# Attention scores from two fp32r parts, with two heads' products side by side in row tiles

## The chip, the cores and the metric

The kernel runs on one core of one Trainium2 chip. The metric is device time in microseconds (us). The kernel before was run three times: median 2558.04 us, from 2553.32 to 2560.26.

## The reference

Input x is (1, 4096, 256) in float32. The work is one attention block and one feed-forward block:

```python
# n = 4096 tokens, d = 256, H = 16 heads, hd = 16
def attn(x):
    qkv = x @ w_attn + b_attn                       # 256 -> 768
    q, k, v = split(qkv), each to (b, H, n, hd)
    logits = einsum('bhqd,bhkd->bhqk', q, k) * hd ** -0.5
    logits = where(causal, logits, -inf)
    out = einsum('bhqk,bhkd->bhqd', softmax(logits), v)
    return out @ w_proj + b_proj
def ffn(x):                                         # w1, w2: 1024x256, h1, h2: 1024x1024, w3: 256x1024
    h = silu(tlin(x, w1)) * tlin(x, w2)
    h = gelu(tlin(h, h1)); h = gelu(tlin(h, h2))
    return tlin(h, w3)
x = x + layernorm(attn(layernorm(x)))
x = x + layernorm(ffn(layernorm(x)))
```

Softmax subtracts the largest logit of each row; the kernel computes that largest logit first, with products of its own.

## The kernel before

**Tiling.** The tokens are cut into 8 chunks of 512 (`CW`), the 16 heads into 4 groups of 4 (`NG`, `GH`). A unit is one group and one chunk of 512 queries; there are 32 units, in the order of `UNITS`. Unit (g, c) has `4c + 4` steps, one for each tile of 128 keys: 576 steps in all. In the last four steps of a unit, the masked ones, only the last 512, 384, 256 and 128 query columns are computed.

**A step** on TensorE (PE) is: for each of 4 heads one score product S (L533, keys as weights, queries streaming) into one of three PSUM banks 0 to 2 (`STB`); in a masked step also a 128-column product that adds the mask (L539); then, for the step before, 4 value products (L495), one for each head, in column tiles of 32, each of which the trace shows as two instructions. A score product waits until the exponential (ScalarE, L1020) of three products earlier has emptied its bank.

**Queries and keys** come in three bf16 parts each. Six products of parts are stacked along the contraction: `KPART` and `QPART`, 96 rows, and 3 more rows (`ROWS`) that subtract the row maximum, itself in three bf16 parts. The parts are made on ScalarE (L966, L972) and VectorE (L731, L735, L738), written to DRAM as `qk_parts` and read back by 6 DMAs for each load of keys (`load_k`) or queries (`load_q`).

**Pieces.** The row maxima need the same logits with queries as weights. A piece is one such product (L460) of 128 queries of one head and up to 512 keys, into one of four banks 3 to 6 (`MXB`, `take`), and one VectorE instruction that takes its maximum: L753 for a full piece, or for one on the diagonal L759, which adds the mask and takes the maximum. A piece waits until the maximum of four pieces earlier has been taken. There are 2304 pieces, 512 of them on the diagonal. When a unit's pieces are done, `row_max` turns the maxima (a transpose on PE, L469), splits them, and SyncE sends them through DRAM (`row_max`) into the last rows of the queries.

**Order.** All engines follow one static order. `beats()` gives, for five points of each step (before the first head and after each head), how many "c" calls (work on a chunk: layer norm, transposes, projections of q, k, v) and how many "p" calls (pieces) come there; `row_max_times()` sets when pieces are due, with `RATE`, `LEAD`, `LEAD_END` and `PIECE`. Each engine is a queue in order: a piece that waits on PE holds back the score products and value products behind it. In the first group of heads the chunk work runs beside the steps. Weight splitting for the feed-forward block (L991, L996 on ScalarE, L1111 on GpSimd) runs beside the later steps. GpSimd otherwise sets constants and computes `rstd` (L1101). SyncE issues every DMA.

**After the attention** the feed-forward block runs on PE in fp32r (L616, L623, L661, L669). The change does not touch it.

## Time and profile before

| | |
|---|---|
| profiled execution, own time | 2552.76 us |
| its span | 2551.0 us |
| mean granted TensorE clock | 0.970 |
| PE busy | 94% |
| VectorE (DVE) busy | 72% |
| ScalarE (ACT) busy | 59% |
| GpSimd (POOL) busy | 4% |

The span goes from the first to the last instruction. Busy is the union of an engine's instructions; matmuls are pipelined, so that the duration of one holds its latency and the distance between two starts is what it occupies. A granted clock of 1.00 is 2.4 GHz, of 0.50 is 1.2 GHz. The last value product ends at about 1856 us of the span; from there on the feed-forward block runs alone.

### The profile page before, as it was taken

What the parts mean: (1) busy time and instruction counts of PE and PEld (TensorE: products, weight loads), DVE (VectorE), ACT (ScalarE), POOL (GpSimd) and SP (SyncE); (2) the same over time, 40 slices, a digit from 0 to 9 for tenths busy, and PEclk for the clock granted to TensorE, in tenths of its full rate; (3) what the DMA queues carried; (4) which work ended last, traced back from release to release, by engine and by line L of the source; (5) the groups of instructions that cost most, each with busy time, mean ns of one, the idle gap of its engine ahead of it and who ended that gap; (6) DMA issues with size and microseconds to landing.
All of it is one profiled execution on the core that took longest, in us unless ns stands there. A gap on an engine that the chain in (4) does not pass through costs nothing.

```text
span 2551.0 us, 36168 instructions
## 1 busy us (share of the span) xinstructions
PE 2405.5 (94%) x13346; PEld 1141.1 (45%) x13346; DVE 1826.5 (72%) x3926; ACT 1505.3 (59%) x2965; POOL 104.4 (4%) x87
## 2 busy tenths in 40 slices
PE   6699999899999999999999999999989999999998
PEld 3233333222332333333333222332368888888887
DVE  7789888898888888888888787876634354434442
ACT  3145557566777777777777777777644344433442
POOL 3000000000000000000000000000000000000000
PEclk9689999899999999999999999999999999999999
DMA  4421101100121111222111000002111011101100
GB/s 125 123 57 47 47 1 53 37 26 18 53 62 39 39 31 34 57 65 63 58 53 51 18 13 10 10 10 79 32 32 35 1 35 35 35 1 35 34 9 9
DMA packets 90293, 99.88 MB, mean 39 GB/s; under 512 B 18208, under 2 KB 70176, under 8 KB 90112
## 3 DMA queue, kind: packets, MB, share of 16 engines
q1 hardware_dynamic: 90112, 97.53, 13.4%
q8 instruction: 106, 1.74, 0.3%
q14 instruction: 75, 0.61, 0.1%
HBM read 59.85 MB, written 37.62 MB: 38 GB/s over the span
## 4 chain that ended last, share of the span: by engine, by line
PE 79%; DVE 10%; issue 4%; SPq 2%; DMA 2%; ACT 2%; POOL 0%; DVEq 0%; POOLq 0%
PE ps L495 19%; PE ps L533 18%; PE ps L460 16%; PE ps L616 10%; PE ps L623 10%; DVE mp L753 5%; DVE ps L759 2%; SPq L1123 2%; PE ps L434 1%; ACT r L1020 1%; DMA qk_parts<-r 1%; PE ps L661 1%; PE ps L669 1%; PE ps L539 1%; PE ps L603 1%
## 5 line engine op out<-in xcount | busy, mean ns | idle before, releaser
L1020 ACT ACTIVATE r<-ps 128x512 f32<-128x512 f32 (+3 forms) x2304 | 1133.5, 567 | 533.5 <-PE ps L533 321.0
L753 DVE TENSOR_REDUCE mp<-ps 128x1 f32<-128x512 f32 x1792 | 1135.6, 683 | 177.7 <-PE ps L460 171.1
L460 PE MATMUL ps<-r,r 96*128 96x512 bf16 (+3 forms) x2304 | 841.1, 374 | 17.3 <-DVE mp L753 8.4
L533 PE MATMUL ps<-r,r 99*128 99x512 bf16 (+3 forms) x2304 | 820.4, 368 | 22.5 <-ACT r L1020 10.6
L495 PE MATMUL ps<-r,V 128*17 128x512 f32 (+2 forms) x4608 | 575.7, 572 | 0.0
L533 PEld LDWEIGHTS ps<-r,r 99*128 99x128 bf16 x2304 | 223.9, 98 | 669.4 <-ACT r L1020 477.9
L460 PEld LDWEIGHTS ps<-r,r 96*128 96x128 bf16 x2304 | 227.3, 99 | 251.0 <-DVE mp L753 64.3
L759 DVE CUSTOM_DVE_ANT_0 ps<-ps,mask_q 128x128 f32<-128x128 f32 (+3 forms) x512 | 255.4, 499 | 94.2 <-PE ps L460 39.3
L616 PE MATMUL ps<-har,wres 128*128 128x512 f32 x512 | 202.1, 395 | 0.0
L623 PE MATMUL ps<-har,wres 128*128 128x512 f32 x512 | 199.5, 390 | 0.0
L623 PE MATMUL ps<-hbr,h2r 128*128 128x512 f32 x512 | 199.2, 389 | 0.0
L616 PE MATMUL ps<-hbr,h2r 128*128 128x512 f32 x512 | 199.2, 389 | 0.0
L866 DVE TENSOR_TENSOR har<-ps,har 128x512 fp32r<-128x512 f32 x128 | 87.9, 686 | 147.9 <-ACT har L1034 147.4
L495 PEld LDWEIGHTS ps<-r,V 128*17 128x17 f32 x4608 | 76.6, 95 | 204.0 <-issue 200.1
L866 DVE TENSOR_TENSOR hbr<-ps,hbr 128x512 fp32r<-128x512 f32 x64 | 44.3, 692 | 158.7 <-ACT hbr L1034 158.7
L1062 ACT ACTIVATE ps<-ps,tail 128x512 f32<-128x512 f32 x64 | 42.4, 662 | 161.4 <-PE ps L623 161.4
L1070 ACT ACTIVATE ps<-ps,tail 128x512 f32<-128x512 f32 x64 | 42.4, 662 | 150.0 <-PE ps L623 150.0
L539 PE MATMUL ps<-mask_k,idb 128*128 128x128 bf16 x512 | 108.8, 223 | 0.0
L616 PEld LDWEIGHTS ps<-har,wres 128*128 128x128 f32 x512 | 96.1, 188 | 20.1
L623 PEld LDWEIGHTS ps<-har,wres 128*128 128x128 f32 x512 | 96.1, 188 | 20.1
L623 PEld LDWEIGHTS ps<-hbr,h2r 128*128 128x128 f32 x512 | 96.1, 188 | 19.9
L616 PEld LDWEIGHTS ps<-hbr,h2r 128*128 128x128 f32 x512 | 96.1, 188 | 19.9
(87 smaller groups left out, 1673.8 us busy)
## 6 DMA issues: line engine op xcount, KB each, us to landing
r<-qk_parts SPq DMA_DIRECT2D x384, 64.0 KB, 2.9
qk_parts<-r SPq DMA_DIRECT2D x24, 512.0 KB, 5.1
low_h<-wst SPq DMA_DIRECT2D x32, 256.0 KB, 2.1
r<-in_x SPq DMA_DIRECT2D x8, 512.0 KB, 5.2
attn_out<-tail SPq DMA_DIRECT2D x128, 32.0 KB
tail<-in_h1t SPq DMA_DIRECT2D x16, 256.0 KB, 3.0
tail<-in_h2t SPq DMA_DIRECT2D x16, 256.0 KB, 3.2
h_hi<-wst SPq DMA_DIRECT2D x16, 256.0 KB, 2.5
```

What stands on the lines that cost most here:

```text
L460: e.matmul(bank[:, 0:wide], QS[0:ROWS, u % SLOTS, h, 128 * qt:128 * qt + 128], KS[0:ROWS, g % 2, h, CW * k:CW * k + wide], start=True, sto ...
L495: mm_ = e.matmul(ps[32 * h:32 * h + HD + 1, OUB, off:CW], V[:, kt, GH * g + h, :], PB[:, (4 * step + h) % PBN, off:CW], start=(kt == 0), s ...
L533: mm_ = e.matmul(bank[:, off:CW], KS[0:ROWS + 3, g % 2, h, 128 * kt:128 * kt + 128], QS[0:ROWS + 3, u % SLOTS, h, off:CW], start=True, sto ...
L539: mm_ = e.matmul(bank[:, off:off + 128], idb[:, :], mask_k[:, :], start=False, stop=True)
L616: e.matmul(bank, W[:, k, ms], src[0][:, k, :], start=(k == 0), stop=False)
L623: mm_ = e.matmul(bank, W[:, k, ms], src[1][:, k, :], start=False, stop=(k == nk - 1))
L753: e.tensor_reduce(dst, bank[:, 0:wide], AX.X, ALU.max).then_inc(s_mx, 1)
L759: e.tensor_tensor_reduce(bank[:, 0:wide], bank[:, 0:wide], mask_q[:, 512 - wide:512], 1.0, LOWEST, ALU.add, ALU.max, dst).then_inc(s_mx, 1)
L866: e.tensor_tensor(dst[1][:, m, :], bank, dst[0][:, m, :], ALU.subtract).then_inc(s_sq, 1)
L1020: e.activation(PB[:, n % PBN, off:CW], ps[:, STB[n % len(STB)], off:CW], ACT.Exp, scale=HD ** -0.5).then_inc(s_ex, 1)
L1062: e.activation(bank, bank, ACT.Gelu, scale=G1[:, m:m + 1]).then_inc(s_hb, 1)
L1123: return e.dma_start(dst, src)
```

## The change

Queries and keys are kept in two fp32r parts; three products of parts are stacked, 48 rows, and 2 rows of ones and row maximum. Two heads of a group lie at partitions 0 and 64, and their products are issued with `tile_position=(64 * j, 0)`. A piece now covers two heads: two products into two neighbouring banks (two slots of two banks instead of four of one), and one maximum over both. The mask of a diagonal piece is added by a 128-column product for each head, in place of the VectorE instruction. In a step the scores go in two pairs. The low part of q and k is computed on GpSimd; ScalarE makes the sum with the bias twice. The planner's constants, the number of calls and the places of the DMAs follow.

```diff
-LEAD = 5.0
+LEAD = 6.0
 LEAD_END = 9.0
-PIECE = 0.6
+PIECE = 1.2
 STB = [0, 1, 2]
-MXB = [3, 4, 5, 6]
+MXB = [3, 5]
...
 
-KPART = [0, 0, 1, 0, 2, 1]
-QPART = [0, 1, 0, 2, 0, 1]
-ROWS = 96
+KPART = [0, 0, 1]
+QPART = [0, 1, 0]
+ROWS = 48
 
 UNITS = [(g, c) for g in range(NG) for c in ORDERS[g]]
...
 ORDER = list(range(NC - 1, -1, -1))
-AHEAD_CALLS, CHUNK_CALLS = 14, 23
+AHEAD_CALLS, CHUNK_CALLS = 13, 7
...
 
 
 def stages():
 
-    for n in range(8):
-        if n < 4:
-            yield "qk", n
-        if n in (4, 6):
-            yield "v", n - 4
-        if 1 <= n < 5:
-            yield "first", n - 1
-        if 2 <= n < 6:
-            yield "rest", n - 2
-        if 3 <= n < 7:
-            yield "second", n - 3
-        if 4 <= n < 8:
-            yield "third", n - 4
+    for n in range(4):
+        yield "qk", n
+    yield "v", 0
+    yield "v", 2
 
 
...
-        mp = sb("mp", [128, 2, 16, NC])
+        mp = sb("mp", [128, 2, GH, 4, NC])
...
-        m1 = sb("m1", [16, 3, 128], BF)
-        mr = sb("mr", [16, 128])
+        m1 = sb("m1", [16, 2, 128], FR)
...
                 return r, bank_of[what]
 
...
             def pieces():
                 n = 0
                 for u, (g, c) in enumerate(UNITS):
-                    for h in range(GH):
+                    for p in range(2):
                         for qt in range(4):
                             for k in range(c + 1):
                                 wide = CW if k < c else 128 * (qt + 1)
                                 w.wait_ge(s_ql[u % SLOTS], 96 * (u // SLOTS + 1))
                                 w.wait_ge(s_kl[g], 96 * (k + 1))
                                 r, bank = take(("piece", n))
-                                e.matmul(bank[:, 0:wide],
-                                         QS[0:ROWS, u % SLOTS, h, 128 * qt:128 * qt + 128],
-                                         KS[0:ROWS, g % 2, h, CW * k:CW * k + wide], start=True,
-                                         stop=True).then_inc(s_ap, 1)
+                                for j in range(2):
+                                    rows = slice(64 * j, 64 * j + ROWS)
+                                    mm_ = e.matmul(
+                                        bank[:, j, 0:wide],
+                                        QS[rows, u % SLOTS, p, 128 * qt:128 * qt + 128],
+                                        KS[rows, g % 2, p, CW * k:CW * k + wide], start=True,
+                                        stop=k < c, tile_position=(64 * j, 0))
+                                if k == c:
+                                    w.wait_ge(s_c, 3)
+                                    w.wait_ge(s_g, 2)
+                                    for j in range(2):
+                                        mm_ = e.matmul(bank[:, j, wide - 128:wide], idb[:, :],
+                                                       mask_q[:, :], start=False, stop=True)
...
+                    beat(3 * step)
                     off = 128 * max(0, kt - 4 * c)
-                    for h in range(GH):
-                        n = 4 * step + h
-                        bank = ps[:, STB[n % len(STB)], :]
-                        w.wait_ge(s_ex, n + 1 - len(STB)) if n >= len(STB) else None
-                        w.wait_ge(s_mr[u % SLOTS], 16 * (u // SLOTS + 1))
+                    for p in range(2):
+                        w.wait_ge(s_mr[u % SLOTS], 32 * (u // SLOTS + 1))
                         w.wait_ge(s_ql[u % SLOTS], 96 * (u // SLOTS + 1))
                         w.wait_ge(s_kl[g], 96 * (kt // 4 + 1))
-                        w.wait_ge(s_g, 6)
-                        if g % 2:
-                            w.wait_ge(s_ko, 1)
-                        mm_ = e.matmul(bank[:, off:CW],
-                                       KS[0:ROWS + 3, g % 2, h, 128 * kt:128 * kt + 128],
-                                       QS[0:ROWS + 3, u % SLOTS, h, off:CW], start=True,
-                                       stop=kt < 4 * c)
+                        n = 4 * step + 2 * p
+                        for j in range(2):
+                            rows = slice(64 * j, 64 * j + ROWS + 2)
+                            if n + j >= len(STB):
+                                w.wait_ge(s_ex, n + j + 1 - len(STB))
+                            mm_ = e.matmul(ps[:, STB[(n + j) % len(STB)], off:CW],
+                                           KS[rows, g % 2, p, 128 * kt:128 * kt + 128],
+                                           QS[rows, u % SLOTS, p, off:CW], start=True,
+                                           stop=kt < 4 * c, tile_position=(64 * j, 0))
+                            if kt < 4 * c:
+                                mm_.then_inc(s_sT, 1)
                         if kt >= 4 * c:
                             w.wait_ge(s_c, 3)
-                            mm_ = e.matmul(bank[:, off:off + 128], idb[:, :], mask_k[:, :],
-                                           start=False, stop=True)
-                        mm_.then_inc(s_sT, 1)
-                        beat(5 * step + h + 1)
+                            w.wait_ge(s_g, 4)
+                            for j in range(2):
+                                e.matmul(ps[:, STB[(n + j) % len(STB)], off:off + 128], idb[:, :],
+                                         mask_k[:, :], start=False, stop=True).then_inc(s_sT, 1)
+                        beat(3 * step + p + 1)
                     if late is not None:
                         values(*late)
...
-                    if kind == "rest":
-                        w.wait_ge(s_p1, 4 * c + f + 1)
-                        e.tensor_tensor(T0[b][:, f, :], T0[b][:, f, :], TP[b][0][:, f, :],
-                                        ALU.subtract).then_inc(s_p2, 1)
-                    if kind == "second":
-                        w.wait_ge(s_p2, 4 * c + f + 1)
-                        e.tensor_copy(TP[b][1][:, f, :], T0[b][:, f, :]).then_inc(s_p3, 1)
-                    if kind == "third":
-                        w.wait_ge(s_p3, 4 * c + f + 1)
-                        e.tensor_tensor(TP[b][2][:, f, :], T0[b][:, f, :], TP[b][1][:, f, :],
-                                        ALU.subtract).then_inc(s_p4, 1)
                     yield
...
-                                bank = bank_of["piece", n]
-                                dst = mp[:, u % 2, 4 * h + qt, k:k + 1]
                                 w.wait_ge(s_ap, n + 1)
-                                if k < c:
-                                    e.tensor_reduce(dst, bank[:, 0:wide], AX.X,
-                                                    ALU.max).then_inc(s_mx, 1)
-                                else:
-                                    w.wait_ge(s_g, 2)
-                                    if n:
-                                        w.wait_ge(s_mx, n)
-                                    e.tensor_tensor_reduce(
-                                        bank[:, 0:wide], bank[:, 0:wide], mask_q[:, 512 - wide:512],
-                                        1.0, LOWEST, ALU.add, ALU.max, dst).then_inc(s_mx, 1)
+                                e.tensor_reduce(mp[:, u % 2, 2 * p:2 * p + 2, qt, k],
+                                                bank_of["piece", n][:, :, 0:wide], AX.X,
+                                                ALU.max).then_inc(s_mx, 1)
...
-                w.wait_ge(s_ms, 5 * u + 2)
-                e.scalar_tensor_tensor(out=mr[:, :], in0=bank[0:16, 0:128], scalar=-1.0,
-                                       in1=m1[:, 0, :], op0=ALU.mult,
+                w.wait_ge(s_ms, 3 * u + 2)
+                e.scalar_tensor_tensor(out=m1[:, 1, :], in0=bank[0:16, 0, 0:128], scalar=-1.0,
+                                       in1=m1[:, 0, :].bitcast(F32), op0=ALU.mult,
                                        op1=ALU.subtract).then_inc(s_ms, 1)
-                w.wait_ge(s_ms, 5 * u + 3)
-                e.tensor_copy(m1[:, 1, :], mr[:, :]).then_inc(s_ms, 1)
-                w.wait_ge(s_ms, 5 * u + 4)
-                e.tensor_tensor(m1[:, 2, :], mr[:, :], m1[:, 1, :],
-                                ALU.subtract).then_inc(s_ms, 1)
...
                         if c >= 2:
-                            w.wait_ge(s_p4, 4 * (c - 2) + 4)
-                        e.activation(T0[b][:, f, :], bank_of["qk", c, f], ACT.Identity,
-                                     bias=ba[:, f:f + 1]).then_inc(s_t0, 1)
-                    if kind == "first":
-                        w.wait_ge(s_t0, 4 * c + f + 1)
-                        if c >= 2:
-                            w.wait_ge(s_scr[b], 48 * (c // 2))
-                        e.copy(TP[b][0][:, f, :], T0[b][:, f, :]).then_inc(s_p1, 1)
+                            w.wait_ge(s_scr[b], 32 * (c // 2))
+                        bank = bank_of["qk", c, f][:, 0, :]
+                        e.activation(TP[b][:, 1, f, :].bitcast(F32), bank, ACT.Identity,
+                                     bias=ba[:, f:f + 1])
+                        e.activation(TP[b][:, 0, f, :], bank, ACT.Identity,
...
-            e.memset(r1[ROWS:ROWS + 3, 0:8192], ONES).then_inc(s_g, 1)
-            w.wait_ge(s_g, 5)
+            for n, rows in enumerate((slice(32, 64), slice(96, 128))):
...
+                for _ in range(6):
+                    yield
+                root(c)
+                w.wait_ge(s_pw, c + 1)
+                if c == 0:
+                    for n, rows in enumerate((slice(32, 64), slice(96, 128))):
+                        w.wait_ge(s_g, 7 + n)
+                        e.memset(KS[rows, 0, :, CW:T].bitcast(F32), 1.0).then_inc(s_g, 1)
+                    w.wait_ge(s_g, 9)
+                if c == 1:
+                    for n, rows in enumerate((slice(32, 64), slice(96, 128))):
+                        if n:
+                            w.wait_ge(s_ko, n)
+                        e.memset(KS[rows, 1, :, :].bitcast(F32), 1.0).then_inc(s_ko, 1)
+                    w.wait_ge(s_ko, 2)
+
+            def projected(c):
+                for kind, f in stages():
+                    if kind == "qk":
+                        w.wait_ge(s_hi, 4 * c + f + 1)
+                        if c or f:
+                            w.wait_ge(s_lo, 4 * c + f)
+                        low = TP[c % 2][:, 1, f, :]
+                        e.tensor_tensor(low, low.bitcast(F32), TP[c % 2][:, 0, f, :].bitcast(F32),
+                                        ALU.subtract).then_inc(s_lo, 1)
+                    yield
+
+            for _ in inputs(turned, projected):
+                pass
+            w.wait_ge(s_lo, 4 * NC)
...
-                            "(h d) t -> d h t", d=HD)).then_inc(s_kl[g], 16)
+                for j in range(2):
+                    for i in range(3):
+                        first = 64 * j + 16 * i
+                        dma(KS[first:first + 16, g % 2, :, c * CW:(c + 1) * CW],
+                            scr[KPART[i], D + 64 * g:D + 64 * g + 64, c * CW:(c + 1) * CW]
+                            .rearrange("(h j d) t -> j d h t", j=2, d=HD)[j]).then_inc(s_kl[g], 16)
 
...
-                w.wait_ge(s_p4, 4 * c + 4)
-                for i in range(3):
+                w.wait_ge(s_lo, 4 * c + 4)
+                for i in range(2):
                     dma(scr[i].rearrange("(f p) t -> p f t", p=128)[:, :, c * CW:(c + 1) * CW],
-                        TP[c % 2][i]).then_inc(s_scr[c % 2], 16)
+                        TP[c % 2][:, i, :, :]).then_inc(s_scr[c % 2], 16)
                 load_k(0, c)
                 load_q(c)
-                load_k(1, c)
+                for n in range(c - 2, c + 1 if c == NC - 1 else c - 1):
+                    if n >= 0:
+                        load_k(1, n)
 
```

## Rows read from the trace of the kernel before

**Rows 1.** The page: chain that ended last, share of the span by line.

```profile
PE ps L495 19%; PE ps L533 18%; PE ps L460 16%; PE ps L616 10%; PE ps L623 10%; DVE mp L753 5%; DVE ps L759 2%; SPq L1123 2%; PE ps L434 1%; ACT r L1020 1%; DMA qk_parts<-r 1%; PE ps L661 1%; PE ps L669 1%; PE ps L539 1%; PE ps L603 1%
```

**Rows 2.** Busy time by stretch: stretch, length, engines (instructions), clock, DMA share, GB/s.

```profile
340.00:360.00 20.00, 20.00 (x104) 7.56 (x101) 14.85 (x31) 14.21 (x28) 0.00 (x0) 1.00 0.00 1
360.00:380.00 20.00, 16.01 (x59) 4.60 (x56) 18.83 (x42) 3.90 (x8) 0.00 (x0) 0.76 0.01 1
```

**Rows 3.** The same view for the score products, L533, alone.

```profile
0.00:400.00 400.00, 94.00 (x260) 25.74 (x260) 0.88 0.25 70
400.00:800.00 400.00, 189.15 (x518) 50.32 (x517) 0.97 0.13 36
800.00:1400.00 600.00, 304.34 (x856) 83.34 (x856) 0.99 0.17 49
1400.00:1870.00 470.00, 232.88 (x672) 64.47 (x672) 0.98 0.08 25
```

**Rows 4.** The same view for the pieces' products, L460, alone.

```profile
0.00:400.00 400.00, 153.35 (x383) 38.54 (x384) 0.88 0.25 70
400.00:800.00 400.00, 204.65 (x565) 55.50 (x565) 0.97 0.13 36
800.00:1400.00 600.00, 294.36 (x826) 81.19 (x826) 0.99 0.17 49
1400.00:1870.00 470.00, 188.73 (x531) 52.01 (x530) 0.98 0.08 25
```

**Rows 5.** Timeline of a step without pieces (start, us, engine, line, operation).

```profile
1834.96 0.82 PE L533 MATMUL ps<-r,r 99*128 99x512 bf16 x3
...
1835.39 2.06 ACT L1020 ACTIVATE r<-ps 128x512 f32<-128x512 f32 x4 [1.30 <-PE ps L533]
...
1836.04 0.39 PE L533 MATMUL ps<-r,r 99*128 99x512 bf16 x1 [0.26 <-ACT r L1020]
...
1836.36 1.05 PE L495 MATMUL ps<-r,V 128*17 128x512 f32 x8
...
1837.35 0.82 PE L533 MATMUL ps<-r,r 99*128 99x512 bf16 x3
```

**Rows 6.** Timeline of PE in a step with four pieces.

```profile
1002.61 0.39 PE L533 MATMUL ps<-r,r 99*128 99x512 bf16 x1
...
1004.09 0.38 PE L460 MATMUL ps<-r,r 96*128 96x512 bf16 x1
```

**Rows 7.** Timeline of VectorE beside such steps.

```profile
1008.06 0.70 DVE L759 CUSTOM_DVE_ANT_0 ps<-ps,mask_q 128x512 f32<-128x512 f32 x1
...
1008.86 2.48 DVE L753 TENSOR_REDUCE mp<-ps 128x1 f32<-128x512 f32 x4
```

**Rows 8.** Timeline of fp32r products in the feed-forward block.

```profile
1943.80 0.28 PE L661 MATMUL ps<-wres,har 128*128 128x256 f32 x1
1943.92 0.28 PE L669 MATMUL ps<-wres,har 128*128 128x256 f32 x1
...
2100.03 0.39 PE L623 MATMUL ps<-hbr,h2r 128*128 128x512 f32 x1
2100.03 0.19 PEld L616 LDWEIGHTS ps<-hbr,h2r 128*128 128x128 f32 x1
2100.25 0.39 PE L616 MATMUL ps<-hbr,h2r 128*128 128x512 f32 x1
```

**Rows 9.** Groups of instructions over the span (count, busy us, mean ns).

```profile
L731 DVE TENSOR_TENSOR r<-r 128x512 f32<-128x512 f32 x32 | 21.8, 682 | 11.3 <-ACT r L972 11.3
L886 DVE TENSOR_TENSOR late<-late 128x1024 f32<-128x1024 f32 x8 | 9.8, 1225 | 0.3
```

**Rows 10.** Timeline of the start.

```profile
2.56 6.92 POOL L1091 MEMSET r<- 3x8192 f32 x1
...
11.85 5.70 DVE L692 TENSOR_SCALAR ve<-mv 128x4 f32<-128x4 f32 x1
...
113.82 0.61 PE L533 MATMUL ps<-r,r 99*128 99x512 bf16 x1 [9.09 <-DMA r<-row_max]
```

More of the change, by code:

```diff
@@ L175, in inputs @@
             yield
-            next(ahead, None)
+            for _ in range(3):
+                next(ahead, None)
         yield
@@ L549, in tensor_program @@
                         r, bank = take("flag")
-                        e.matmul(bank[0:1, 0:1], accs[:, :], one[:, :], start=True,
+                        e.matmul(bank[0:1, 0, 0:1], accs[:, :], one[:, :], start=True,
                                  stop=True).then_inc(s_fl, 1)
```

214 lines of the change are left out of this document (105 added, 109 removed).

## The prediction, made before the changed kernel ran

> **What bounds the kernel now.** I read the table by stretch first, then the chain of waits, the groups by shape, and timelines of single steps. The chain is PE nearly throughout: values 19%, scores 18%, pieces 16% of the span [rows 1]. The feed-forward block after 1856 us is untouched and its about 695 us stay. Of the 576 steps, 65 (260 products over 4) lie before 400 us and 511 after [rows 3]; from 400 to 1400 us there are 343.5 steps of 2.91 us with 1391 pieces, 4.05 per step, then 3.2 per step [rows 3, 4]. In the first 400 us two limits alternate: at 340 to 360 PE is busy all the time, at 360 to 380 DVE is (18.8 of 20 us) and PE waits for it at a granted clock of 0.76 [rows 2].
>
> Two timelines say what a step is made of. With four pieces: first to last of the 8 products 1.48 us, 0.21 us a start [rows 6]. Without pieces: three scores at once, exponentials from 0.43 us on, the fourth score only at 1.08 us, because it waits for the first exponential to empty its bank; 0.32 us to the values, 0.99 us for them, 2.39 us in all [rows 5]. So PE work is not the only thing in a step: even with no pieces at all it costs 2.39 us, by a loop through ACT (score, exponential, fourth score, values). ACT needs 2.06 us for four exponentials [rows 5].
>
> **The change, part by part.**
>
> *Score pairs.* The wait of the fourth score stays: three banks, the same condition. Halving the scores' PE time therefore saves nothing below 1.08 us; it only frees room inside the wait.
>
> *Piece pairs.* The calls of a step are now before, between and after two pairs; the first place gets nothing, since the point before it has the same time. So about half the pieces come between the pairs, inside the wait, and cost nothing as long as their slot is free; half come after the fourth score, and each delays the values. What does a pair cost PE? No row shows row tiles. If both run together it is one fp32r product, 0.225 us a start [rows 8]; if the second begins only when the first ends, 0.45 us. Two weight loads must fit as well: 256-column products with a load each start every 0.12 us [rows 8], so two loads are at most 0.24 us. I take 0.24: the four values, in column tiles, 8 instructions of 512 columns, take 1.05 us in all [rows 5], against 8 x 0.21 = 1.7 us if they ran one after another, so tiles do run together on this array.
>
> The Trainium skill, "TensorE: Matmul & The Clock Gate", part 3 on packing, says that matmuls in different row groups overlap, starting about 4 ns apart, and that a weight load overlaps a running matmul only when its row group differs. The first half would give the low end, 0.225 to 0.24 us a pair. The second half is not what this trace shows: a load of the full array starts with the running product, both at 2100.03 us [rows 8].
>
> *Masks of pieces.* 256 of the 1152 pairs get two 128-column products more. At 0.21 us for 512 columns these are 0.05 us each; and the tile mode changes twice. A change costs about 0.10 us by [rows 5] (0.32 us from the last score to the values against 0.21 to a next product). Together 0.30 us; per piece 256/1152 of it, 0.07 us. In masked steps the score pairs change mode too, 0.1 to 0.2 us in a step, against about 0.2 us that the paired first scores save; I set these equal.
>
> The Trainium skill, "TensorEngine Tiling (Array Packing)", Key Properties, says that changing the mode drains TensorE. It speaks against masks that sit between row-tiled products. Had each change to wait for a whole latency (0.39 us less its 0.21 us of columns [rows 6], 0.18 us), 256 masked pieces would cost another 2 x 0.08 us each, half of them hidden: 20 us more.
>
> *VectorE.* Four plain maxima take 2.48 us, so one follows another in 0.60 us; masked ones of 512 columns need 0.80 us (1008.06 to 1008.86) [rows 7], of 320 columns on average about 0.60. A maximum over 2x512 columns is not shown: 0.60 us plus 512 columns more. An instruction over 1024 columns has a mean of 1225 ns against 682 ns for 512 [rows 9], 0.54 us more: 1.14 us. Bounds are 0.6 (columns at double rate) and 1.23. So 2304 x 0.60 = 1382 us becomes 896 x 1.14 + 256 x 0.74 = 1211 us. Three operations on the parts go to GpSimd, of which 32 of 682 ns are one [rows 9]; all three make about 57 us, at 682, 682 and 417 ns. Per unmasked step at 2.17 pairs DVE has 2.17 x 1.05 = 2.3 us of work, below the 2.7 us that I find for the step: it isn't the bound, but it is near it.
>
> *Slots.* Two slots of two banks in place of four of one: a third piece of a step (about one step in six has three) waits up to 0.4 us for its slot, and the values wait behind it. I put 0.05 us on the average step; bounds 0 and 0.3.
>
> *Sum over the steps from 400 us on.* Where pieces are dense, 4.35 a step: before (3 + 4.35) x 0.215 = 1.58 us up to the last product. After: 1.08 + 1.09 x 0.24 + 1.09 x 0.07 + 0.05 = 1.47 us. That is 0.11 to 0.12 us less of a step of 2.9 us. The 1922 pieces from 400 us on [rows 4] fill 442 such steps: **-53 us**. Most of the PE time removed is not gained, because the wait for the first exponential takes its place.
>
> *First 400 us.* Pieces on DVE: 383 [rows 4], 230 us before, 192 x 1.05 = 202 after, -28; the three part operations behind 100 us, -35. On PE (260 + 383)/2 x 0.21 = -68 us, masks 50 x 0.3 = +15. Either limit is relieved by 50 to 60 us of the 286 us from 114 to 400; as they alternate and the value and projection work stays, I take **-45 us**, bounds -15 and -70.
>
> *Start.* The first score waits until 113.8 us for the row maximum, which went through SyncE's queue behind chunk 3's loads [rows 10]; in the new order 18 loads still stand ahead of it (12 for chunks 0 and 1, since the next group's keys come two chunks later). Against that, GpSimd now clears 7168 columns twice after the first `rstd` and 8192 columns twice after the second, at 6.9 us for 8192 [rows 10]: 12 and 14 us, and the second pair lies before the last low part of chunk 0, whose write to DRAM starts about 8 us later. While such a memset ran, a 4-column operation on DVE took 5.70 us [rows 10]; the normalisation of chunk 0 can be held like that. The shorter loads (6 x 0.5 us each for two chunks) return about as much. **+4 us**, bounds -8 and +20.
>
> *ACT and DMA.* ACT's chunk work stays (two sums in place of a sum and a copy). DMA bytes grow by a third for the parts, at a share of 0.25 in the first 400 us and 0.17 later [rows 3]; nothing, and up to 5 us in the start if not hidden.
>
> Together -53 - 45 + 4 = -94 us: 2552.8 of the profiled execution becomes 2459; the median of the runs shown is 5.3 us above that execution, so **2464 us**.
>
> **Rivals.**
>
> *A: forecast*, 2464, own range 2420 to 2515. Chance 0.50.
>
> *B: the pieces vanish wholly beside ACT*, also those after the fourth score: steps fall to 2.39 us, 0.5 x 442 = -221 us, first part -65: about 2275. For it: DVE's 2.3 us would allow it. Against: the values stand in the same queue behind the piece. 0.08.
>
> *C: the pairs don't overlap* (weight loads or waits keep them apart), so the change doesn't do what it says. A pair is 0.45 us: 1.08 + 1.09 x (0.45 + 0.07) + 0.05 = 1.70 against 1.58, +53 us; the first 400 us gain nothing, start +4: about 2612, slower. It decides from 0.35 us a pair on, where the steps break even. For it: no row-tiled product in the trace, each half waits for its own bank's exponential, and two heads' exponentials end 0.5 us apart; against it: the column tiles of [rows 5]. 0.18.
>
> *D: the two long slots couple PE to DVE.* If each piece after the fourth score waits 0.2 us more, 1.09 x 0.2 x 442 = +97 us cancel the gain: about 2560. For it: 1.14 us is longer than the way from one piece to the next; DVE would be 80 to 85% busy. 0.15.
>
> *E: the granted clock falls to its lower level more often*, as at 360 to 380 us where PE waited [rows 2]. At 1.2 GHz a step's products and values take about 1.6 us more; in 50 steps +80 us: about 2545. For it, PE has more gaps; against it, a step without pieces had three quarters of its time filled. 0.09.
>
> A measurement of this kernel can tell about 0.3% (8 us) from no change. Faster: A, B, and a third of D and half of E, 0.68. Within 0.3%: 0.06. Slower: C and the rest, 0.26. The range 2380 to 2610 leaves out B and the upper half of C.
>
> **What would show it.** Right: unmasked steps of 2.7 to 2.8 us with pieces and 2.4 without; starts of the two products of a piece pair under 0.12 us apart and pairs 0.24 apart; the fourth score still released by an exponential at 1.08 us; a maximum of 1.2 us each, DVE 80% busy from 400 us on; attention's end near 1760 us. Wrong: pair starts 0.2 us apart or more (C); PE waiting for maxima by over 0.1 us a step (D); a clock under 0.93 in the stretches from 400 us on (E); a first score after 130 us.

## The result: 2925.5 us, slower by 14%

The changed kernel takes 2925.52 us (median of 4 runs, 2895.13 to 2965.76), the kernel before 2556.16 us in the same call. The ratio is 1.140, 95% interval 1.131 to 1.150. The medians here and below are over all runs, while the ratios leave out those more than 1.5% above the fastest of the same kernel (here the one at 2965.76 us). Forecast were 2464 us, at most 2610. Below, "pieces" are L448 (their mask products L457), scores L528 (masks L538), values L491, maxima L735, the transpose of the row maxima L465, exponentials L991.

First the page of the changed kernel:

```profile
span 2917.0 us, 34936 instructions
...
PE 2690.8 (92%) x13858; PEld 1325.8 (45%) x13858; DVE 1694.7 (58%) x2102; ACT 1506.6 (52%) x2957; POOL 158.6 (5%) x123
...
PEclk8777788667979976996899976876576999999999
...
L735 DVE TENSOR_REDUCE mp<-ps 128x2 f32<-128x1024 f32 (+3 forms) x1152 | 1284.5, 1135 | 708.0 <-PE ps L448 542.8
```

PE is still busy nearly all the time, and no other engine has come near it. What is new is the third line shown, the granted clock in tenths: digits of 5 to 8 among the nines over the whole attention, which ends at 2221 us instead of 1855. The feed-forward block keeps its 695 us, with nines. All of the +366 us of span is in the attention.

The next view answers to [rows 3], the scores by stretch; columns are stretch, length, PE, PEld, granted clock, DMA share, GB/s:

```profile
0.00:400.00 400.00, 69.35 (x214) 33.28 (x215) 0.80 0.23 71
400.00:800.00 400.00, 153.81 (x428) 67.81 (x426) 0.80 0.12 33
800.00:1400.00 600.00, 253.69 (x716) 110.00 (x716) 0.85 0.15 42
1400.00:1870.00 470.00, 212.74 (x588) 89.18 (x587) 0.88 0.09 28
1870.00:2230.00 360.00, 146.11 (x362) 64.47 (x361) 0.65 0.08 24
```

By 400 us there are 53.5 steps done instead of 65, and afterwards the clock is 0.65 to 0.88 where it was 0.97 to 0.99.

**At full clock.** A step with two pairs of pieces, all engines (it answers to [rows 5, 6]):

```profile
1851.84 0.19 PEld L528 LDWEIGHTS ps<-qs,ks 50*128 50x128 f32 x2 [0.85 <-ACT pb L991]
1851.84 0.50 PE L528 MATMUL ps<-qs,ks 50*128 50x512 f32 x2
...
1852.18 0.39 PE L448 MATMUL ps<-ks,qs 48*128 48x512 f32 x2
...
1852.19 0.19 PEld L528 LDWEIGHTS ps<-qs,ks 50*128 50x128 f32 x1
1852.38 2.06 ACT L991 ACTIVATE pb<-ps 128x512 f32<-128x512 f32 x4 [0.77 <-PE ps L528]
1852.42 0.39 PE L528 MATMUL ps<-qs,ks 50*128 50x512 f32 x1
1852.62 2.41 DVE L735 TENSOR_REDUCE mp<-ps 128x2 f32<-128x1024 f32 x2 [0.43 <-PE ps L448]
...
1853.03 0.50 PE L528 MATMUL ps<-qs,ks 50*128 50x512 f32 x1 [0.23 <-ACT pb L991]
...
1853.03 0.73 PE L448 MATMUL ps<-ks,qs 48*128 48x512 f32 x2
...
1853.69 1.05 PE L491 MATMUL ps<-pb,V 128*17 128x512 f32 x8
...
1854.68 0.49 PE L528 MATMUL ps<-qs,ks 50*128 50x512 f32 x2
```

The two products of a pair run together: in the trace they start less than 0.01 us apart, and each of these two lasts 0.50 us. A pair that is queued behind products of its own tile mode costs 0.23 to 0.24 us (the pieces at 1852.18, the third score at 1852.42). The first scores of a step cost 0.34 us (1851.84 to 1852.18): their weight load starts together with them, and they last 0.50 us where the third score, whose load ran ahead at 1852.19, lasts 0.39. The fourth score lasts 0.50 us as well, and its load starts with it, too. In the kernel before, a score whose load starts with it takes 0.39 us all the same (1836.04, [rows 5]); its bf16 load takes 0.10 us where the fp32r one takes 0.18 to 0.19.

The fourth score waits for an exponential, at 1.19 us of the step. From there it is 0.66 us to the values, because the second pair of pieces stands between, and the step takes 2.84 us. Two steps with four pieces of the kernel before took 2.77 us (1002.61, [rows 6], to its successor at 1005.38; one of its pieces has 384 columns) and 2.84 (1005.38 to 1008.22, all pieces of 512). There is no gain even at full clock. With three pairs it is worse:

```profile
1005.71 0.50 PE L528 MATMUL ps<-qs,ks 50*128 50x512 f32 x2
1006.05 0.63 PE L448 MATMUL ps<-ks,qs 48*128 48x512 f32 x4
...
1007.76 0.50 PE L448 MATMUL ps<-ks,qs 48*128 48x512 f32 x2 [0.38 <-DVE mp L735]
...
1009.18 0.49 PE L528 MATMUL ps<-qs,ks 50*128 50x512 f32 x2
```

Here the first two pairs cost 0.46 us together (1006.05 to 1006.51). The third waits 0.38 us for one of the two slots, and the step takes 3.47 us.

**Where the clock goes.** PE around the end of a unit:

```profile
1666.80 0.28 PE L457 MATMUL ps<-mask_q,idb 128*128 128x128 bf16 x2
1668.81 0.27 PE L465 MATMUL ps<-idf,mm 128*16 128x128 f32 x1 [1.73 <-DVE mm L748]
1669.01 1.91 PE L491 MATMUL ps<-pb,V 128*17 128x512 f32 x8
```

PE waits 1.73 us for VectorE to finish the row maxima; the 8 value instructions after it take 1.91 us instead of 1.05. What follows, as busy time of PE, PEld, DVE, ACT and POOL with the granted clock behind them:

```profile
1655.00:1665.00 10.00, 9.35 (x63) 3.04 (x60) 8.34 (x8) 7.75 (x16) 1.28 (x1) 1.00 0.08 27
1669.00:1673.00 4.00, 3.74 (x13) 0.94 (x12) 0.56 (x2) 1.33 (x3) 0.00 (x0) 0.50 0.04 8
1673.00:1680.00 7.00, 7.00 (x27) 1.71 (x26) 0.00 (x0) 2.92 (x6) 0.00 (x0) 0.50 0.16 41
1680.00:1690.00 10.00, 10.00 (x48) 3.54 (x46) 0.00 (x0) 4.46 (x13) 1.26 (x1) 0.50 0.00 0
1690.00:1700.00 10.00, 10.00 (x44) 4.29 (x40) 5.94 (x5) 6.21 (x12) 0.00 (x0) 0.50 0.31 80
1700.00:1710.00 10.00, 10.00 (x39) 3.21 (x42) 4.92 (x6) 5.47 (x12) 0.00 (x0) 0.50 0.01 2
```

The same view of the kernel before, around its own unit end at 1622.1 us:

```profile
1622.00:1626.00 4.00, 3.89 (x18) 1.26 (x19) 1.05 (x4) 2.08 (x4) 0.00 (x0) 0.64 0.03 6
1626.00:1630.00 4.00, 4.00 (x32) 1.43 (x29) 2.65 (x4) 2.86 (x7) 0.00 (x0) 0.93 0.00 0
1630.00:1640.00 10.00, 10.00 (x81) 3.90 (x74) 7.54 (x16) 7.49 (x20) 0.00 (x0) 1.00 0.19 51
```

This is the point of the case. The wait and the fall of the clock are in both kernels: the 32 waits sum to 55.7 us before and 53.8 after. The kernel before is back at full clock within some 5 us. The changed one stays at 0.50 (1.2 GHz) for 40 us and more, with PE busy 10.00 of 10. I read the clock behind every unit end from 400 us on. Before, it was lowered in 9 of 26 cases and at full speed again 4 to 7 us after the transpose in all but one. After, it was low behind 22 of 27 (at three of these it was, or had just been, at 0.50 already), and in 14 of them still at 0.50 to 0.60 in the stretch 17 to 27 us later. The falls themselves sit at the unit ends: from 400 us to the end of the attention 9 of 10 falls begin within 2 us of such a transpose before, and 20 of 22 after. Summed up, the clock is at 0.50 for 41 us of this stretch before and for 699 us after.

**Account of the +366 us.** I divided span by busy time of the exponentials, in windows of 5 us from 400 us on; I call this the pace. Windows with a clock of at least 0.95: 1.504 after (1045 us of them), 1.418 before (1380 us). Windows at 0.55 or less: 2.390 after (625 us of them; before only 5 us). After 400 us the changed kernel spends 1821 us on 1025 us of exponentials. At its own full-clock pace these would take 1541, so the clock accounts for 280 us. Before, 1455 us went to 1005 us of exponentials, 1.448 for each. The same sum gives 30 us lost to the clock there ((1.448 - 1.418) times 1005). So of the +366 us some 250 are clock. The slower pace at full clock (1.504 against 1.418, times 1005) makes 86, and the 20.5 us more of exponentials that are left over from the first 400 us make 31. This is an estimate: it takes it that the windows of either clock hold the same mix of steps.

**The start.** VectorE, then GpSimd (it answers to [rows 10]):

```profile
12.59 13.03 DVE L708 TENSOR_SCALAR r<-r,mv,rstd 128x256 f32<-128x256 f32 x4 [1.23 <-POOL rstd L1054]
...
40.43 15.76 DVE L708 TENSOR_SCALAR r<-r,mv,rstd 128x256 f32<-128x256 f32 x4 [12.87 <-POOL rstd L1054]
```

```profile
12.62 12.22 POOL L1080 MEMSET ks<- 32x7168 f32 x2
...
40.45 13.93 POOL L1086 MEMSET ks<- 32x8192 f32 x2
```

Each time the four normalisations last about as long as the memsets beside them. The first score comes at 130.5 us, 16.7 later than before.

### The profile page after: what moved, and what is told of

The parts are those of the page before. It is cut to its first block, busy times and chain, and to the rows that moved or that the text cites. A ratio compares the mean times of both kernels' runs of the same rounds, so it can differ in the third digit from the quotient of the medians.

```text
span 2917.0 us, 34936 instructions
## 1 busy us (share of the span) xinstructions
PE 2690.8 (92%) x13858; PEld 1325.8 (45%) x13858; DVE 1694.7 (58%) x2102; ACT 1506.6 (52%) x2957; POOL 158.6 (5%) x123
## 4 chain that ended last, share of the span: by engine, by line
PE 80%; ACT 6%; DVE 6%; issue 4%; DMA 1%; SPq 1%; POOL 0%; POOLq 0%; DVEq 0%
PE ps L491 22%; PE ps L528 21%; PE ps L448 10%; PE ps L614 9%; PE ps L621 9%; ACT pb L991 6%; DVE mp L735 5%; PE ps L538 2%; PE ps L457 2%; PE ps L422 2%; SPq L1121 1%; PE ps L659 1%; PE ps L667 1%; DMA qk_parts<-parts 1%; PE ps L601 1%
## 5 line engine op out<-in xcount | busy, mean ns | idle before, releaser
L735 DVE TENSOR_REDUCE mp<-ps 128x2 f32<-128x1024 f32 (+3 forms) x1152 | 1284.5, 1135 | 708.0 <-PE ps L448 542.8
L991 ACT ACTIVATE pb<-ps 128x512 f32<-128x512 f32 (+3 forms) x2304 | 1127.8, 565 | 860.3 <-PE ps L528 521.3
L528 PE MATMUL ps<-qs,ks 50*128 50x512 f32 (+3 forms) x2304 | 835.7, 535 | 67.9 <-ACT pb L991 62.3
L528 PEld LDWEIGHTS ps<-qs,ks 50*128 50x128 f32 x2304 | 364.7, 217 | 877.4 <-ACT pb L991 577.4
L448 PE MATMUL ps<-ks,qs 48*128 48x512 f32 (+3 forms) x2304 | 678.2, 488 | 34.0 <-DVE mp L735 27.4
L491 PE MATMUL ps<-pb,V 128*17 128x512 f32 (+2 forms) x4608 | 696.0, 683 | 0.0
L448 PEld LDWEIGHTS ps<-ks,qs 48*128 48x128 f32 x2304 | 303.0, 221 | 121.4 <-DVE mp L735 59.7
L491 PEld LDWEIGHTS ps<-pb,V 128*17 128x17 f32 x4608 | 80.2, 100 | 187.6 <-issue 176.3
L614 PE MATMUL ps<-xtr,wres 128*128 128x512 f32 x256 | 101.1, 395 | 1.5 <-DVE xtr L846 1.5
L621 PE MATMUL ps<-xtr,wres 128*128 128x512 f32 x256 | 100.9, 394 | 0.0
```

Source lines behind the costliest of these rows:

```text
L448: mm_ = e.matmul(bank[:, j, 0:wide], QS[rows, u % SLOTS, p, 128 * qt:128 * qt + 128], KS[rows, g % 2, p, CW * k:CW * k + wide], start=True ...
L491: mm_ = e.matmul(ps[32 * h:32 * h + HD + 1, OUB, off:CW], V[:, kt, GH * g + h, :], PB[:, (4 * step + h) % PBN, off:CW], start=(kt == 0), s ...
L528: mm_ = e.matmul(ps[:, STB[(n + j) % len(STB)], off:CW], KS[rows, g % 2, p, 128 * kt:128 * kt + 128], QS[rows, u % SLOTS, p, off:CW], star ...
L614: e.matmul(bank, W[:, k, ms], src[0][:, k, :], start=(k == 0), stop=False)
L621: mm_ = e.matmul(bank, W[:, k, ms], src[1][:, k, :], start=False, stop=(k == nk - 1))
L735: e.tensor_reduce(mp[:, u % 2, 2 * p:2 * p + 2, qt, k], bank_of["piece", n][:, :, 0:wide], AX.X, ALU.max).then_inc(s_mx, 1)
```

## The experiments

Theories: **R**, products that fill few rows of the array do not bring the clock back; **G**, the shorter gaps within the steps, of which the changed kernel has more, keep it low. **S** is the full-clock step (slots, maxima, place of the pieces), apart from the clock.

### 1. The kernel before with 48 rows

```diff
-QS[0:ROWS, ...], KS[0:ROWS, ...]            # pieces, 96 rows
-KS[0:ROWS + 3, ...], QS[0:ROWS + 3, ...]    # scores, 99 rows
+QS[0:48, ...], KS[0:48, ...]
+KS[0:48, ...], QS[0:48, ...]
```

> The kernel before, with every score product and every piece contracted over 48 rows instead of 99 and 96 (the other parts and the row maximum are left out of the logits); same instructions, columns, waits and weights otherwise, no row tiles. Theory R (the granted clock falls because products that fill few rows of the array do not hold it up): clock of the attention under 0.9, 2650 to 2900 us. Theory G (the clock falls because the changed kernel leaves PE idle for more of a step, whatever the rows): PE has the same columns and gaps as before, so 2556 us within 0.5%, clock 0.97.

3861.85 us, ratio 1.510 (1.508 to 1.513). The kernel leaves the other parts and the row maximum out of the logits; no instruction was added, no wait changed.

```profile
1000.00:2000.00 1000.00, 986.78 (x3205) 222.81 (x3207) 497.98 (x969) 455.68 (x841) 30.34 (x24) 0.50 0.10 27
2000.00:3000.00 1000.00, 989.86 (x3186) 220.36 (x3178) 472.02 (x867) 453.80 (x820) 13.89 (x11) 0.50 0.05 15
3200.00:3250.00 50.00, 50.00 (x227) 41.57 (x226) 17.90 (x47) 15.88 (x26) 2.01 (x2) 1.00 0.00 1
```

PE is busy 987 and 990 us of 1000, at half clock for 2000 us on end. The third line is from the feed-forward block of the same run, whose products fill 128 rows: there the clock is 1.00. The effect is far larger than R expected (2650 to 2900 us), since in the attention almost nothing brings the clock back. In this kernel, busy time alone does not decide the clock; how many rows the products fill counts too.

The Trainium skill, "TensorE: Matmul & The Clock Gate", part 1, says that the gate is set by how busy PE has recently been, and lists the busy state with the full clock. By that rule these stretches would run at 1.00. The trace disagrees, with 0.50.

### 2. The kernel before with gaps instead

```diff
+cols = wide if n % 2 == 0 else 1
-e.matmul(bank[:, 0:wide], QS[...], KS[..., CW * k:CW * k + wide], ...)
+e.matmul(bank[:, 0:cols], QS[...], KS[..., CW * k:CW * k + cols], ...)
```

> The kernel before, with the product of every second piece cut to one column (its maximum is still taken over the full width, of what the bank holds); rows stay 96 and 99. PE loses about 1150 x 0.2 us of columns, VectorE nothing. Theory G: the clock falls to 1.2 GHz in long stretches as in the changed kernel, mean under 0.9, 2600 us or more. Theory R: clock stays 0.95 or more, and steps fall toward 2.5 to 2.6 us, where VectorE holds them: 2430 to 2500 us.

2465.27 us, ratio 0.964 (0.962 to 0.966), with every second piece's product cut to one column.

```profile
1000.00:1700.00 700.00, 661.37 (x4440) 200.53 (x4441) 592.29 (x1241) 552.75 (x1151) 24.51 (x20) 0.98 0.15 43
```

PE is idle 5.5% of this stretch (6.5% in the changed kernel at 1655 to 1665 us), 1.3% in experiment 1, and the clock holds. G falls. This says nothing against the longer waits at the unit ends, where the falls begin. The gain shows what less PE work in the steps is worth when the clock stays: 92 us for 1152 products.

### 3. The changed kernel with all rows, one product after the other

```diff
-rows = slice(64 * j, 64 * j + ROWS)         # pieces; scores likewise, with + 2
+rows = slice(0, 64 + ROWS)                  # 112 rows, 114 for scores
-stop=k < c, tile_position=(64 * j, 0))
+stop=k < c)
```

> The changed kernel without row tiles: both products of each pair run over rows 0 to 112 or 114, both heads' parts together (so the logits are sums of two heads), one after another on the whole array. Theory R and theory G both give a clock of 0.95 or more. At full clock a step then costs about 0.45 us for each of the late piece and 0.2 us more at the first pair: 3.1 us, attention 576 x 3.1 = 1790 us, in all about 2650 us: less than the changed kernel's 2925, if the clock is what costs most. If the two-slot coupling to VectorE is the cause (theory D), it stays above 2850.

2803.60 us, ratio 1.096 (1.094 to 1.098): 122 us less than the changed kernel although its pairs no longer overlap. It computes sums over both heads. The clock of the span is 0.970, as both theories had it, but the time is 150 us above the 2650 expected.

```profile
1855.06 0.73 PE L528 MATMUL ps<-qs,ks 114*128 114x512 f32 x2
...
1855.64 0.63 PE L448 MATMUL ps<-ks,qs 112*128 112x512 f32 x2
...
1857.14 1.05 PE L491 MATMUL ps<-pb,V 128*17 128x512 f32 x8
...
1858.13 0.50 PE L528 MATMUL ps<-qs,ks 114*128 114x512 f32 x1
```

The step takes 3.07 us against 2.84 with tiles, so the tiles do save 0.23 us in such a step. The 3.1 us expected came true for this step and not for the average: at full clock the pace is 1.623, where this step has 3.07 over 2.06 us of exponentials, 1.49. Only 20 us are low. The overlap is worth having; what the changed kernel loses by its clock is more.

### 4. The changed kernel with maxima over half the columns

```diff
-bank_of["piece", n][:, :, 0:wide], AX.X,
+bank_of["piece", n][:, :, 0:wide // 2], AX.X,
```

> The changed kernel with each maximum taken over the left half of each bank: VectorE's work for pieces falls from 1.16 to about 0.62 us each. Theory D (PE waits for the slots): full-clock steps fall from 3.17 to 2.85 us, 110 us over 378 steps, and more where the clock follows, 2700 to 2810 us. Theories R and G: at most 30 us less, 2890 us or more, since the clock still falls at the unit ends.

2800.72 us, ratio 1.094 (1.092 to 1.097), clock 0.881. The pace at full clock only goes from 1.504 to 1.481, 24 us over 1025; the low windows shrink from 625 to 405 us, and that is most of the 125 us gained. The time lies in the range that was expected if the slots couple PE to VectorE (2700 to 2810 us) and not in that of R and G (2890 or more). The way there is another one, though: the full-clock step did not fall by the 0.3 us that this needs. What the shorter maxima shorten are the waits at which the clock falls: the 32 at the unit ends sum to 36.5 us instead of 53.8, those for a slot to 2.6 instead of 27.4. So VectorE's longer maximum costs little in itself and much by the clock.

### 5. The changed kernel with 64 rows in each tile

```diff
-rows = slice(64 * j, 64 * j + ROWS)         # scores: + ROWS + 2
+rows = slice(64 * j, 64 * j + 64)
+e.memset(QS[part_, :, :, :].bitcast(F32), 0.0)   # once: rows 32 to 63 and 96 to 127
```

> The changed kernel with each row-tiled product contracted over all 64 rows of its tile (the 14 or 16 rows beyond 50 or 48 of the queries are zeros, set once at the start); same instructions, columns and waits. Theory R (rows filled hold the clock up; shown for 48 against 96 rows without tiles): 128 rows in place of 100 while a pair runs, clock in the attention from 0.81 up to 0.9 or more, 2700 to 2850 us. If row tiles themselves are what doesn't count, the clock stays and so does the time, 2900 to 2950 us.

2746.43 us, ratio 1.072 (1.070 to 1.074), clock 0.928. The rows added hold zeros on the query side; the result of every product is the same and no instruction on PE is added. It saves 179 us. The low windows from 400 us on go from 625 to 190 us, the full-clock pace stays (1.491). This is R at work in the changed kernel itself, and it also says that the zeros count.

### 6. The changed kernel with products that nobody reads

```diff
+e.matmul(bank[:, 0, :], KS[:, g % 2, p, CW * k:CW * k + 128],
+         KS[:, g % 2, p, CW * k:CW * k + CW], start=True, stop=True)
 # one before each piece between the score pairs, six before each L465
```

> The changed kernel plus products that nobody reads: one of 512 columns over all 128 rows ahead of each piece that lies between the two score pairs (PE waits there 0.65 us for the first exponential), and six while PE waits for the last maxima of a unit. Theory R and the finding that the clock falls in the wait at the unit ends: mean clock of the attention 0.93 or more, most of the 280 us of the low clock come back less some 30 us for the fillers: 2650 to 2720 us, faster by added work. If only the ratio of idle time counted, one product of 0.22 us in 2.8 us would change little: 2880 us or more.

2792.95 us, ratio 1.092 (1.089 to 1.094), clock 0.948. More work on the engine that is busy 92% of the span makes the kernel 133 us faster, though not the 205 to 275 us that were expected. Low windows: 120 us. Pace at full clock: 1.525, so that the products cost a little where the clock was high anyway.

### 7. The changed kernel with all pieces between the score pairs

```diff
 for p in range(2):
-    advance(step + (p + 1) / 2)
+    advance(step + 1)
```

> The changed kernel with all calls of a step (pieces and chunk work) moved between the two score pairs, so that none stands between the fourth score and the values. At full clock the step should fall from 2.83 to about 2.60 us (the late piece's 0.24 us goes into the 0.65 us wait), unless the second piece must wait for its slot (theory D), which would then hold back the third score. Fewer gaps also help the clock. 2750 to 2850 us; if the slots bind, 2900 or more.

2733.83 us, ratio 1.068 (1.066 to 1.070), clock 0.895.

```profile
1602.08 0.50 PE L528 MATMUL ps<-qs,ks 50*128 50x512 f32 x2
...
1602.42 0.76 PE L448 MATMUL ps<-ks,qs 48*128 48x512 f32 x4
...
1603.02 0.75 PE L528 MATMUL ps<-qs,ks 50*128 50x512 f32 x2
...
1603.69 1.05 PE L491 MATMUL ps<-pb,V 128*17 128x512 f32 x8
...
1604.68 0.50 PE L528 MATMUL ps<-qs,ks 50*128 50x512 f32 x2
```

With both pairs inside the wait for the exponential, the step takes 2.60 us, and the full-clock pace is 1.379, below the 1.418 of the kernel before. So S has a cure: the second pair of pieces stood in front of the values. At full clock a gain of the forecast's kind is there: 0.039 times 1005, 39 us against the kernel before, where 53 were forecast. It has a price in waits: those of pieces for a slot sum to 65.8 us instead of 27.4, those at the unit ends to 65.4 instead of 53.8. Low windows still take 360 us.

### 8. The changed kernel with the ones set chunk by chunk

```diff
-e.memset(KS[rows, 0, :, CW:T].bitcast(F32), 1.0)      # c == 0
-e.memset(KS[rows, 1, :, :].bitcast(F32), 1.0)         # c == 1
+e.memset(KS[rows, 0, :, CW * c:CW * c + CW].bitcast(F32), 1.0)   # every c
+e.memset(KS[rows, 1, :, CW * c:CW * c + CW].bitcast(F32), 1.0)
```

> The changed kernel with the rows of ones set chunk by chunk on GpSimd (about 1 us each, four in each of eight chunks) in place of two memsets of 6.1 and two of 7.0 us. The four normalisations of chunks 0 and 1 that the memsets held for 13.0 and 15.8 us should take 2 to 5 us, and the first score comes at about 112 to 116 us in place of 130.5: 15 to 20 us less in all, near the spread of this kernel's runs (2895 to 2966).

2885.88 us, ratio 1.125 (1.121 to 1.130). The first score comes at 118.3 us instead of 130.5 (expected were 112 to 116), so that 12 of the 17 us at the start are the memsets'. The rest of the difference is not told apart from the scatter of this kernel (2865.72 to 2912.55).

### 9. Experiments 5, 7 and 8 together

> The changed kernel with three edits together: 64 rows in each tile (pad64), all calls of a step between the pairs (mid), the ones set chunk by chunk (spread_ones). If rows and gaps both act on the clock and the edits add, the clock of the attention is 0.95 or more; with mid's full-clock pace (1.38 us per us of exponentials from 400 us on, 1020 us of them) 1410 us there, 695 behind, about 440 before: 2530 to 2590 us, level with the kernel before. If the clock stays near 0.9: 2650 or more.

2652.24 us, ratio 1.030 (1.022 to 1.038), clock 0.933. The four runs scatter more than those of any other kernel here: 2615.74, 2651.45, 2653.03 and 3212.72 us, the last at a clock of 0.638. This is the outcome expected for a clock that stays low; the 2530 to 2590 us expected at 0.95 did not come. Together the edits win back 273 us of the 369; one by one it was 179, 192 and 40, so they overlap in part.

### 10. And six unread products in each unit-end wait

```diff
 r, bank = take(("rows", u))
+for _ in range(6):
+    e.matmul(bank[:, 0, :], KS[:, g % 2, p, CW * k:CW * k + 128],
+             KS[:, g % 2, p, CW * k:CW * k + CW], start=True, stop=True)
 w.wait_ge(s_ms, 3 * u + 1)
```

> combo plus six unread products of 512 columns over 128 rows in PE's wait at each unit's end. The clock falls first in that wait; if this is what starts the low stretches that are left, the clock reaches 0.97 and the time falls 20 to 60 us below combo; if not, it rises by up to 10 us.

2586.22 us, ratio 1.012 (1.009 to 1.014), clock 0.971.

```profile
1631.80 0.28 PE L457 MATMUL ps<-mask_q,idb 128*128 128x128 bf16 x2
1632.83 1.67 PE L465 MATMUL ps<-ks 128*128 128x512 f32 x6 [0.74 <-DVE mp L741]
1634.34 0.27 PE L469 MATMUL ps<-idf,mm 128*16 128x128 f32 x1
...
1634.97 1.05 PE L495 MATMUL ps<-pb,V 128*17 128x512 f32 x8
```

In the place of 1.73 us of waiting stand 0.74 us and six products, and the values behind them take 1.05 us: the clock has not fallen. The transpose stands 2.54 us behind the last mask product instead of 2.01, so each unit end pays 0.53 us, 17 us for 32 of them. Even so it takes 66 us less than experiment 9 by the medians, and 30 us less than the fastest run of it.

### 11. The same without the mask products of the pieces

> combo_filled without the mask products of the diagonal pieces (the row maximum is then taken over keys behind the diagonal too, which only shifts the softmax by another constant). 512 products of 128 columns and two changes of tile mode for each of 256 pieces go: by 0.3 us each, when half are on the path 40 us less than combo_filled, all of them 77 us, none 0.

2567.49 us (10 runs), ratio 1.006 (1.004 to 1.008), the mask of the diagonal pieces left out. The 512 mask products and their changes of tile mode cost 19 us in this order of pieces (the slowest of the ten runs, 2584.17 us, is hardly below experiment 10). This is the fastest version of the change, and it leaves part of the work out; the kernel before is still 0.6% faster.

### 12. Experiment 10 with 48 and 50 rows again

> The changed kernel with the calls of a step between the score pairs, the ones set chunk by chunk and six unread full-row products in each unit-end wait for the row maximum: the version that took 2586 us, less its 64 rows in each tile (48 in pieces, 50 in scores again). If it is enough to fill the waits at the units' ends (these start every fall of the clock), the clock stays near 0.97 and the time is within 15 us of 2586. If the rows filled within the steps matter too, because the clock also falls inside units or does not come back after the first 400 us, the clock is 0.91 to 0.95 and the time 2640 to 2740 us.

2612.34 us, ratio 1.021 (1.018 to 1.024), clock 0.951. From 400 us on, busy time by engine and the clock, experiment 10 first, this one second:

```profile
400.00:1850.00 1450.00, 1365.36 (x8999) 533.30 (x9003) 1088.46 (x1063) 1058.39 (x2176) 56.15 (x44) 0.99 0.13 39
```

```profile
400.00:1850.00 1450.00, 1370.68 (x8831) 532.87 (x8827) 1074.78 (x1036) 1042.24 (x2141) 56.19 (x44) 0.96 0.13 38
```

It lands between the two expectations. Once the waits at the units' ends are filled, few rows in the steps cost only 26 us more. The two causes work together: the clock falls at the longer waits, and the rows bear on how long it stays low.

## Why the prediction was wrong

*Chosen: forecast A, a faster kernel. What happened: rival E, at several times its size.* The failed step is the one on the granted clock. E was put at 0.09 and at 50 low steps for 80 us, because "a step without pieces had three quarters of its time filled". This argued from PE's busy time. Experiments 1 and 2 show that busy time was not the quantity that decides here: gaps within the steps leave the clock at 0.98, 48 rows hold it at 0.50. The low clock cost about 280 us, 250 more than in the kernel before, and the stretches from 400 us on had 0.65 to 0.88, under the 0.93 that the prediction named as the sign of E. The rows to see it were at hand in part: [rows 2] showed 0.76 in a stretch in which PE waited, the trace of before has a fall of the clock behind 9 of 26 unit ends, and the change halves the rows of every score and piece. Nothing in the trace of before showed a product with 48 rows, and this unknown should have widened the range upward.

*The step at full clock* was the second miss. Forecast: 2.7 to 2.8 us on average, 0.12 us less than before. For the step shown above, with one late pair and no mask, the forecast's terms give 1.08 plus 0.24 up to the start of the last product, 1.32 us, and 2.63 in all. Measured: 1.53 (1853.69 less the 0.32 of [rows 5], less 1851.84) and 2.84. The price of a pair was right, 0.23 to 0.24 us. What was put at nothing is that an fp32r product whose weight load starts with it lasts 0.50 us and not 0.39. This counts twice: the first exponential comes at 0.54 us instead of 0.43, which moves the fourth score from 1.08 to 1.19, and the fourth score itself holds up what follows by 0.11 us. Together this is the 0.21 us. The pieces between the pairs are free, as forecast; experiment 7 put all of them there and got 2.60 us. Instead of -53 us the step made the 86 us of the account. How much of that is steps with three pairs was not counted.

*Slots* were given 0.05 us a step, and that was right: PE's waits for a maximum in front of a piece sum to 27.4 us in 67 waits, over 576 steps 0.05 us each, though a three-pair step can lose 0.38. *Rival D* therefore did not happen as it was described; its sign was more than 0.1 us a step. That VectorE matters all the same, by the clock, is what experiment 4 shows. *Rival C* fell: the products of a pair start together, and experiment 3, where they don't overlap, has a step of 3.07 us.

*The maximum* was right: forecast 1.14 us between two, here 1.18 to 1.2 (2.41 us for two). VectorE is busy 63% from 400 us on instead of 80%, because everything takes longer.

*Masks of pieces*: 256 times 0.30, half hidden, was about 35 us in the forecast's own terms (0.07 times 1.09 times 442). Experiment 11 gives 19, with all pieces between the score pairs.

*Start*: +17 instead of +4, inside its bounds. The prediction saw in one row (5.70 us for 4 columns) that a memset can hold VectorE, and named the normalisation of chunk 0; the normalisations of two chunks were held, and the sum has no term for VectorE being held. *First 400 us*: -45 forecast; 11.5 steps fewer were done, with a clock of 0.80 against 0.88 and the late start.

What stays open: whether the rows of each product matter or those of both tiles together; experiments 3 and 5 raised both at once. That the changed kernel with two products of 48 to 50 rows side by side is at full clock in 1045 of its 1821 us, and experiment 1 with single ones of 48 almost never, speaks for the sum, but the two differ in type and order as well. Why the clock falls at some unit ends and not at others, with waits of the same length, is not shown. Open too is whether a version of the change beats the kernel before. Experiment 10 lacks 30 us; the start (7: its first exponential comes at 121.6 us, before at 114.6), the masks (19) and the unread products on the path (17, an estimate) are more than that together, but fewer of those products were not tried.

## What to carry to other kernels

Before a product is made shallower, see in the trace how often the granted clock falls and how it comes back, and try the cheap test of experiment 1: contract over fewer rows and change nothing else. If a change saves rows, pad them back with zeros, and fill the waits at which the clock falls with products that nobody reads; here this was worth 179 us and some 30 to 66. Room made inside a wait only helps if the work is put there: with the pieces between the pairs the step fell from 2.84 to 2.60 us, while the waits for slots grew by 38 us over the whole kernel.

## What the chip showed that I had not expected

- The granted clock can stay at 0.50 for 2000 us while PE is busy 99% (experiment 1). Rows whose query side is zero raise it too (experiment 5, 0.849 to 0.928).
- Added products on the busiest engine saved 133 us (experiment 6).
- A memset on GpSimd stretched four 256-column normalisations on VectorE from 1.4 us to 13.0 and 15.8 us, as long as it ran. In experiment 8, with memsets of 512 columns, no normalisation in the first 60 us took over 1.12 us (up to 7.09 before that edit). The Trainium skill, "GPSIMD Engine Reference", in "Specifications", names an SBUF interface that GpSimd shares with VectorE. The trace agrees so far as VectorE gained almost nothing while a memset ran; that it is this interface was not tested by itself.
- An fp32r product of 512 columns whose weight load starts together with it lasts 0.50 us instead of 0.39, row tiles or not (1851.84 in the changed kernel, 1855.06 in experiment 3 to the next start: 0.34 us instead of 0.23). A bf16 one in the kernel before lasts 0.39 us also then ([rows 5]).
- In row tiles the two products of a pair start less than 0.01 us apart. The Trainium skill, "TensorE: Matmul & The Clock Gate", in "Why this matters for your kernels", has at most 4 ns between the starts of products in different row groups; the trace agrees.
